# One scan per slot over two units in a decoder layer's state-space scan stage

## The reference, cut to what matters

```python
x = silu(conv(in_proj @ hidden) + conv_b)          # (4, 512 channels, 512 steps)
dt_low, Bm, Cm = split(x_proj @ x)                 # 16 + 16 + 16 rows
dt = softplus(dt_proj @ dt_low + dt_b)
def step(state, inp):                              # over the 512 time steps
    d, b, c, u = inp
    dA = exp(d[..., None] * A)                     # decay, 16 states per channel
    state = state * dA + (d * u)[..., None] * b[:, None, :]
    return state, einsum('bdn,bn->bd', state, c)
y = (ys + D * x) * silu(z)                         # z: the normed residual stream
```

## Time and profile before

| | us |
|---|---|
| median of three runs | 1161.83 (1160.21 to 1162.95) |
| the profiled execution, its own time | 1163.83 |
| its span, first to last instruction | 1162.1 |
| PE, DVE, ACT, POOL busy in the span | 1067.5, 826.7, 666.0, 678.5 |
| scan stage, first to last scan | 148.7 to 646.7 |

### The profile page before, as it was taken

The page is one execution under the profiler, slowest core; times in us unless marked ns, Lnnn a source line. Parts: engine busy times, 40 slices in busy tenths (PEclk is TensorE's granted clock), DMA queues, the critical chain, the costliest instruction groups (busy, mean ns, idle before and its releaser), DMA issues. The chain is left out here.

```text
span 1162.1 us, 19085 instructions
## 1 busy us (share of the span) xinstructions
PE 1067.5 (92%) x6650; PEld 651.8 (56%) x6650; DVE 826.7 (71%) x1244; ACT 666.0 (57%) x1442; POOL 678.5 (58%) x587
## 2 busy tenths in 40 slices
PE   7999978888888888888888999999999989999994
PEld 3454545656556556656665544444444467777761
DVE  6988689999999999999999486640680134434428
ACT  3767789999999999999999324202011012333320
POOL 3022299999999999999999450202043035555530
PEclk9999979999999999999999999999999989999997
DMA  7310111101111111112231043102225424444229
GB/s 217 93 38 13 27 28 38 37 28 38 37 38 28 38 38 33 33 38 80 85 110 47 1 146 109 73 37 72 73 78 199 166 75 135 135 131 132 75 74 387
DMA packets 51966, 94.75 MB, mean 82 GB/s; under 512 B 9950, under 2 KB 18142, under 8 KB 51872
## 3 DMA queue, kind: packets, MB, share of 16 engines
q1 hardware_dynamic: 44352, 72.82, 19.5%
q0 software_dynamic: 7520, 20.72, 5.7%
HBM read 74.51 MB, written 20.84 MB: 82 GB/s over the span
## 5 line engine op out<-in xcount | busy, mean ns | idle before, releaser
L699 POOL TENSOR_TENSOR w_all<-w_all 128x512 f32<-128x512 f32 x256 | 320.5, 1275 | 16.2 <-POOLq L96 16.2
L925 DVE TENSOR_TENSOR_SCAN w_all<-da,w_all 128x512 f32<-128x512 f32 x256 | 298.1, 1205 | 1.1 <-POOL w_all L699 0.9
L857 ACT ACTIVATE da<-w_all,a_flat 128x512 f32<-128x512 f32 x256 | 180.3, 705 | 2.3 <-DVE w_all L925 1.6
L793 PE MATMUL yb<-ident,w_all 128*128 128x128 f32 x1024 | 160.4, 280 | 20.9 <-DVE acc L933 20.7
L865 ACT ACTIVATE w_all<-sc,neg_max 128x128 f32<-128x128 f32 (+3 forms) x256 | 134.3, 541 | 15.7 <-DVE neg_max L917 14.7
L793 PEld LDWEIGHTS yb<-ident,w_all 128*128 128x128 f32 x1024 | 115.6, 142 | 45.6 <-issue 23.9
L743 PE MATMUL sc<-w_all,attn 32*128 32x384 f32 (+3 forms) x512 | 105.6, 489 | 27.2 <-ACT w_all L865 21.9
L1352 POOL TENSOR_TENSOR w_all<-w_all 128x512 f32<-128x512 f32 x24 | 29.4, 1226 | 156.1 <-ACT w_all L1548 156.1
L874 ACT ACTIVATE w_all<-tb 128x256 f32<-128x256 f32 (+2 forms) x192 | 103.0, 536 | 27.8 <-PE tb L758 27.7
L917 DVE TENSOR_REDUCE neg_max<-sc 128x2 f32<-128x256 f32 (+3 forms) x128 | 104.1, 813 | 19.9 <-PE sc L746 15.8
L1874 DVE COPY attn<-w_all 128x512 f32 x94 | 40.3, 429 | 108.2 <-PE pe L1815 106.7
(11 more groups left out here) (222 smaller groups left out, 1651.4 us busy)
## 6 DMA issues: line engine op xcount, KB each, us to landing
w_all<-b_scratch SPq DMA_DIRECT2D x64, 256.0 KB, 3.3
w_all<-in_w_up SPq DMA_DIRECT2D x16, 512.0 KB, 5.5
w_all<-in_w_down SPq DMA_DIRECT2D x16, 512.0 KB, 6.7
w_all<-sorted_y SPq DMA_DIRECT2D x16, 512.0 KB, 10.0
attn<-in_x SPq DMA_DIRECT2D x4, 1024.0 KB, 6.9
w_all<-in_x SPq DMA_DIRECT2D x16, 256.0 KB, 4.3
norms<-attn SPq DMA_DIRECT2D x4, 1024.0 KB, 4.3
out_dram<-acc SPq DMA_DIRECT2D x16, 256.0 KB, 9.3
```

What stands on the lines that cost most here:

```text
L699: pool.tensor_tensor(dbu[:, k, :], keep["du"][i // N][:, k * T:(k + 1) * T], b_all[i % 2][:, :], ALU.mult).then_inc(pool_dbu.sem, pool_dbu ...
L793: last = pe.transpose(yb[which][:, k * P:(k + 1) * P], state[i % 2][:, k, t * P:(t + 1) * P], ident[:, :])
L857: act.activation(da[unit % 2][:, :], keep["dt"][i // N][:, k * T:(k + 1) * T], ACT.Exp, scale=keep["a_flat"][:, unit % (N * KD):unit % (N ...
L925: dve.tensor_tensor_scan(state[i % 2][:, k, :], da[unit % 2][:, :], dbu[:, k, :], 0.0, ALU.mult, ALU.add).then_inc(dve_scan.sem, dve_scan. ...
```

## The change

The two scan units of a slot become one pair. `weigh`, `scan` and the waits on them count pairs (128), `decay` still counts units (256). Three things change:

- one scan of 1024 steps per slot runs over both units. The element of the decays at step 512 is set to 0 once at the start, by a DVE memset, and `decay` of the second unit writes only its steps 1 to 511, so the second unit starts afresh;
- the decays lie in two sets of two units: set 0 in two neighbouring PSUM banks (`da_bank`), set 1 in SBUF (`da_sb`). Even pairs use PSUM, odd pairs SBUF. A `decay` waits for the scan two pairs before, and ACT's order moves each decay half a slot ahead (three before the loop);
- POOL forms both products of a pair in one instruction of 128 x 1024, with the row of b read twice (a broadcast of 2).

```diff
-        da = [pb(f"da{i}") for i in range(2)]
+        da_bank = ctx.enter_context(nc.psum_tensor("da", [P, 2 * T], F32))
+        da_sb = sb("da_sb", [P, 2 * T])
+        da = [da_bank[:, :], da_sb[:, :]]
...
-        out_bank = [sc[:, 0, :], sc[:, 1, :], da[0][:, :], da[1][:, :]]
+        out_bank = [sc[:, 0, :], sc[:, 1, :], da_bank[:, 0:T], da_bank[:, T:2 * T]]
...  SP
-                sp.wait_ge(pool_dbu.sem, pool_dbu.upto(4 * (i - 2) + 3))
+                sp.wait_ge(pool_dbu.sem, pool_dbu.upto(2 * (i - 2) + 1))
...  GpSimd
-                if unit >= 4:
-                    pool.wait_ge(dve_scan.sem, dve_scan.upto(unit - 4))
-                pool.tensor_tensor(dbu[:, k, :], keep["du"][i // N][:, k * T:(k + 1) * T], b_all[i % 2][:, :], ALU.mult).then_inc(...)
+                if pair >= 2:
+                    pool.wait_ge(dve_scan.sem, dve_scan.upto(pair - 2))
+                pool.tensor_tensor(dbu[:, k:k + 2, :], keep["du"][i // N].rearrange("p (k t) -> p k t", t=T)[:, k:k + 2, :],
+                                   b_all[i % 2].rearrange("p (a t) -> p a t", a=1).broadcast_to([P, 2, T]), ALU.mult).then_inc(...)
...
             weigh(0)
-            weigh(1)
             for g in range(UNITS + 3):
                 if g + 1 < UNITS:
-                    weigh(2 * g + 2)
+                    weigh(g + 1)
                 if 0 <= g - 3 < UNITS:
                     add(g - 3)
-                if g + 1 < UNITS:
-                    weigh(2 * g + 3)
...  TensorE
-                    pe.wait_ge(dve_scan.sem, dve_scan.upto(4 * i + 3))
+                    pe.wait_ge(dve_scan.sem, dve_scan.upto(2 * i + 1))
...  ScalarE, decay(unit)
-                if unit >= 2:
-                    act.wait_ge(dve_scan.sem, dve_scan.upto(unit - 2))
-                act.activation(da[unit % 2][:, :], keep["dt"][i // N][:, k * T:(k + 1) * T], ACT.Exp,
+                if unit < 4 and unit % 2 == 0:
+                    act.wait_ge(dve_zero.sem, dve_zero.upto(pair))
+                if pair >= 2:
+                    act.wait_ge(dve_scan.sem, dve_scan.upto(pair - 2))
+                first = unit % 2
+                act.activation(da[pair % 2][:, first * T + first:(first + 1) * T], keep["dt"][i // N][:, k * T + first:(k + 1) * T], ACT.Exp,
...
             decay(0)
             decay(1)
+            decay(2)
...  in the loop
-                    decay(2 * g + 2)
+                    decay(2 * g + 3)
...
-                if g + 1 < UNITS:
-                    decay(2 * g + 3)
+                if g + 2 < UNITS:
+                    decay(2 * g + 4)
...  VectorE, scan(pair)
-                dve.wait_ge(act_da.sem, act_da.upto(unit))
-                dve.wait_ge(pool_dbu.sem, pool_dbu.upto(unit))
+                dve.wait_ge(act_da.sem, act_da.upto(2 * pair + 1))
+                dve.wait_ge(pool_dbu.sem, pool_dbu.upto(pair))
...
-                dve.tensor_tensor_scan(state[i % 2][:, k, :], da[unit % 2][:, :], dbu[:, k, :], 0.0, ALU.mult, ALU.add).then_inc(...)
+                dve.tensor_tensor_scan(state[i % 2][:, k:k + 2, :].rearrange("p k t -> p (k t)"), da[pair % 2],
+                                       dbu[:, k:k + 2, :].rearrange("p k t -> p (k t)"), 0.0, ALU.mult, ALU.add).then_inc(...)
...
+            for n in range(2):
+                dve.memset(da[n][:, T:T + 1], 0.0).then_inc(dve_zero.sem, dve_zero.tick(n))
...
-                    scan(2 * g)
-                    scan(2 * g + 1)
+                    scan(g)
```

More of the change, by code:

```diff
@@ L632, in mix @@
         act_da, act_p, act_turn, act_cy = [signal("act_" + n) for n in ("da", "p", "turn", "cy")]
-        dve_max, dve_scan, dve_acc, dve_rinv, dve_out = [signal("dve_" + n) for n in ("max", "scan", "acc", "rinv", "out")]
+        dve_max, dve_scan, dve_acc, dve_rinv, dve_out, dve_zero = [signal("dve_" + n) for n in ("max", "scan", "acc", "rinv", "out", "zero")]
         pool_dbu, pool_acc, pool_du, pool_xb = [signal("pool_" + n) for n in ("dbu", "acc", "du", "xb")]
         pe_out = signal("pe_out")
-        out_bank = [sc[:, 0, :], sc[:, 1, :], da[0][:, :], da[1][:, :]]
+        out_bank = [sc[:, 0, :], sc[:, 1, :], da_bank[:, 0:T], da_bank[:, T:2 * T]]
         x1 = keep["x1"][0]
@@ L668, in preload @@
                 if n == 0:
-                    sp.wait_ge(pool_dbu.sem, pool_dbu.upto(3 * N * KD - 1))
+                    sp.wait_ge(pool_dbu.sem, pool_dbu.upto(3 * N * KD // 2 - 1))
                     sp.wait_ge(act_da.sem, act_da.upto(3 * N * KD - 1))
@@ L689, in last_batch, with weigh @@
                 pool.tensor_tensor(du, dt, du, ALU.mult).then_inc(pool_du.sem, pool_du.tick(j))
-            def weigh(unit):
-                i, k = unit // KD, unit % KD
-                if unit == (B - 1) * N * KD:
+            def weigh(pair):
+                i, k = pair // 2, 2 * (pair % 2)
+                if pair == (B - 1) * N * KD // 2:
                     pool.wait_ge(pool_du.sem, pool_du.upto(KD - 1))
@@ L696, in weigh @@
                     pool.wait_ge(s_b_all[i % 2].sem, s_b_all[i % 2].upto(i // 2))
-                if unit >= 4:
-                    pool.wait_ge(dve_scan.sem, dve_scan.upto(unit - 4))
-                pool.tensor_tensor(dbu[:, k, :], keep["du"][i // N][:, k * T:(k + 1) * T], b_all[i % 2][:, :], ALU.mult).then_inc(pool_dbu.sem, pool_dbu.tick(unit))
+                if pair >= 2:
+                    pool.wait_ge(dve_scan.sem, dve_scan.upto(pair - 2))
+                pool.tensor_tensor(dbu[:, k:k + 2, :], keep["du"][i // N].rearrange("p (k t) -> p k t", t=T)[:, k:k + 2, :],
+                                   b_all[i % 2].rearrange("p (a t) -> p a t", a=1).broadcast_to([P, 2, T]), ALU.mult).then_inc(pool_dbu.sem, pool_dbu.tick(pair))
             def add(n):
@@ L802, in project_out @@
                     if n == 2 * KD:
-                        pe.wait_ge(dve_scan.sem, dve_scan.upto(2 * UNITS - 1))
+                        pe.wait_ge(dve_scan.sem, dve_scan.upto(UNITS - 1))
                     last = pe.matmul(out_bank[t], keep["attn"][:, 0, k * T + t * P:k * T + (t + 1) * P], keep["wo"][:, k, :],
@@ L853, in decay @@
             def decay(unit):
-                i, k = unit // KD, unit % KD
-                if unit >= 2:
-                    act.wait_ge(dve_scan.sem, dve_scan.upto(unit - 2))
-                act.activation(da[unit % 2][:, :], keep["dt"][i // N][:, k * T:(k + 1) * T], ACT.Exp,
+                i, k, pair = unit // KD, unit % KD, unit // 2
+                if unit < 4 and unit % 2 == 0:
[4 more added lines that the diff above has]
+                act.activation(da[pair % 2][:, first * T + first:(first + 1) * T], keep["dt"][i // N][:, k * T + first:(k + 1) * T], ACT.Exp,
                                            scale=keep["a_flat"][:, unit % (N * KD):unit % (N * KD) + 1]).then_inc(act_da.sem, act_da.tick(unit))
@@ L917, in top, with scan @@
                 dve.tensor_reduce(neg_max[unit % 2][:, :], sc[:, :, 0:n], AX.X, ALU.max, negate=True).then_inc(dve_max.sem, dve_max.tick(unit))
-            def scan(unit):
-                i, k = unit // KD, unit % KD
-                dve.wait_ge(act_da.sem, act_da.upto(unit))
-                dve.wait_ge(pool_dbu.sem, pool_dbu.upto(unit))
+            def scan(pair):
+                i, k = pair // 2, 2 * (pair % 2)
+                dve.wait_ge(act_da.sem, act_da.upto(2 * pair + 1))
+                dve.wait_ge(pool_dbu.sem, pool_dbu.upto(pair))
                 if k == 0 and i >= 2:
                     dve.wait_ge(pe_y.sem, pe_y.upto(4 * (i - 2) + 3))
-                dve.tensor_tensor_scan(state[i % 2][:, k, :], da[unit % 2][:, :], dbu[:, k, :], 0.0, ALU.mult, ALU.add).then_inc(dve_scan.sem, dve_scan.tick(unit))
+                dve.tensor_tensor_scan(state[i % 2][:, k:k + 2, :].rearrange("p k t -> p (k t)"), da[pair % 2],
+                                       dbu[:, k:k + 2, :].rearrange("p k t -> p (k t)"), 0.0, ALU.mult, ALU.add).then_inc(dve_scan.sem, dve_scan.tick(pair))
             def weigh_c(n):
```

## The result

The changed kernel takes 1244.87 us (median of 4 runs, 1243.18 to 1246.51) against 1161.93 for the kernel before (median of 4): ratio 1.0715, 95% interval 1.0696 to 1.0735, 83 us slower. Its profiled execution spans 1241.4 us. The forecast was 1251 (1228 to 1285).

The account below looks back on a forecast made before the run. In the scan stage, POOL with the odd scan it gives way to becomes the bound: 9.2 us for two slots against 7.8, 64 x 1.4 = +90 on 1163.8, less about 1 and then 2.0, gives 1251 us (1228 to 1285).

Parts of the forecast that it names:

- Where the operands lie: Scan stage: odd scans with both inputs in SBUF and POOL instructions reading SBUF exclude each other whole, whoever is first.
- three instructions of DVE after the stage: L1203, L1205, L1206 after the scan stage: beside two-SBUF-input DVE instructions, POOL's L1352 took 2.43 us instead of 1.041.
- A: Rival in odd scans: the scan doesn't take the shared interface, POOL goes on; 1154 us or no change; chance 0.08.
- The sum: Scan stage, two slots: POOL's 7.16 us plus odd scan's 2.12 less 0.1 make 9.2 against 7.8; +90 us.
- the hidden start: When DVE and POOL exclude each other, about 0.15 us at the start of the waiting instruction is hidden.
- the 2.02 that the sum had: POOL's added time per odd scan: the scan's 2.12 us less 0.1 for POOL's own hidden start.
- POOL as the bound: POOL with the odd scan becomes the bound, busy about 100% of a stage of 585 to 590 us.
- The cover of the other edits: ACT's decays, SP's b row, PE's waits and scan source memory cost 0; two memsets under 0.5 us together.
- B: Rival in odd scans: only the scan's accesses are taken from POOL, costing 1.06 us each; 1189 us; chance 0.08.
- C: Rival: odd scans come just after POOL begins a product; DVE's wait bounds, 9.9 us per two slots; 1296; chance 0.09.
- the 1.8 that DVE could afford: DVE has 7.4 us of its own in two slots of 9.2, so can wait 1.8 in the odd slot.

Follow-up runs that it names:

- run 8: The changed kernel with POOL's addition of cy to acc cut to one column instead of 512; 1189.74 us.
- run 3: The changed kernel's paired scan and product, but one set of decays only, in SBUF, issued where the kernel before had them; 1372.52 us.
- run 4: The same kernel and schedule as run 3, but with the one set of decays in PSUM; 1243.01 us.
- run 7: The changed kernel with its one scan and two sets, but two products of 512 for one of 1024; 1262.27 us.
- run 6: The changed kernel with its sets and paired product, but two scans of 512 instead of one of 1024; 1272.2 us.
- run 5: The kernel of run 4 with ACT issuing both decays of the next pair one after the other; 1223.59 us, ratio 1.0528.

## Why the prediction was right

**Where the operands lie.** It rested on three instructions of DVE after the stage. The prediction calls them two operations (a product and a comparison), but both are the same instruction, TENSOR_TENSOR, and no scan was among them. That a scan does the same was a bet, as the prediction says under A, and it came out. What they showed holds for the scan: 2.28 us alone, exclusive with POOL's products and additions, whole, whoever is first. It is shown now by the 51 odd scans that end 2.15 us after a POOL instruction, by the one-column addition of run 8, and by runs 3 and 4 (129.5 us apart for the memory alone). The Trainium skill, page "SBUF — State Buffer", section "Who interferes with whom", has this rule for VectorE instructions with two SBUF inputs; the runs agree for the scan.

**The sum.** For two slots it said 9.2 us: measured 9.10 ((726.3 - 148.3) / 127 x 2). Of its terms, the scan was put at 2.27 and is 2.28 to 2.29; the product at 2.35 from start to start and is 2.33 (412.74 to 415.07), the addition at 1.23 and is 1.22 to 1.24. With these, 2 x (2.33 + 1.23) + 2.12 - 0.1 = 9.14. The rest is the hidden start. A scan that waited ends 2.15 after POOL's end, so 0.13 of it is hidden, as the sum had within 0.03; but a POOL product that waited ends 2.15 after the scan where it takes 2.36 alone, so 0.21 of it is hidden and not 0.15, and 0.04 would be hidden behind another POOL instruction. That gives 7.12 + 2.15 - 0.17 = 9.10, as measured. The stage was to grow by 90 us and grew by 82.3: 1.31 us for two slots instead of 1.4. POOL's waits inside its instructions come to 64 x 1.95 us (128 products of 3.076 on average instead of 2.364, 64 additions of 1.801 instead of 1.272: 91.1 + 33.9 = 125 us), near the 2.02 that the sum had. Of these 125 us not all became time: without them POOL is busy for 453 us, which is 45 less than the 498 of the old stage, and 125 - 45, with 2 us in which POOL is idle, is the growth.

**POOL as the bound.** It is 99.6% busy, as said, of a stage of 580 us that was to have 585 to 590; a load added in run 7 lengthens the stage, one taken away in run 8 shortens it.

**The cover of the other edits.** ACT and PE were to be under 80% and are at 81% and 82%; neither became the bound. ACT's decay into SBUF takes 721 ns and into PSUM 692, on average 707 against the 705 of before, so the 0 holds. PE's waits were put at 0 more and its busy time was left as it was; both were wrong. Its weight loads waited 40.5 us for scans, against 0.8 before, and its busy time rose by 40 us (below). That this cost nothing rests on POOL being the fuller engine. The Trainium skill, page "VectorE: DVE Perf Modes", section on the TRN2 errata, has a source in SBUF 62 cycles of 0.96 GHz cheaper than one in PSUM, by estimate 65 ns. This isn't seen: the shortest scan from SBUF took 2279 ns, the shortest from PSUM 2267.

**The rivals.** A (the scan stays out of it) and B (only its accesses are taken) fall with the one-column addition that waits 2 us. C (DVE's wait becomes the bound) didn't happen: an odd scan waited 0.74 us on average (3.025 against 2.286), of the 1.8 that DVE could afford. A bound of that kind appears in run 8, once POOL's load is gone, as DVE at 98%, and in run 6.

**What the experiments' expectations missed.** That splitting the scan would change nothing (run 6, 27 us), and what one set in PSUM costs through ACT's order (runs 4 and 5). What a merged scan is worth in PSUM stays open. As a length the scan of 1024 saves DVE 0.04 us a slot (2.29 against the 2.33 of two), where the prediction had 0.06; no run shows what that is worth in time.

## What to carry to other kernels

Before a buffer that a VectorE instruction reads is moved from PSUM to SBUF, count its SBUF inputs. With two of them, the scan here and GpSimd's instructions that read SBUF ran one after the other. GpSimd then lost 64 x 1.95 = 125 us inside its instructions, and what its slack of 45 us didn't absorb became time, for 0.06 us a slot to be gained. Whether one long instruction does less harm than two short ones depends on what GpSimd runs beside it: one scan instead of two was 27 us better beside the long product and 2 us, within the noise, beside two short ones. Look for the damage in the maximum of each line's duration, since no wait shows it.

## What the runs showed of the hardware that was not expected

PE's granted clock fell in the stage: 0.91 of full speed against 0.99, for the same 4122 matmuls, and PE's busy time rose from 437 to 477 us. In windows of 2 us (PE busy with its count, clock, DMA share, GB/s):

```profile
404.00:406.00 2.00, 0.45 (x2) 0.87 0.00 0
406.00:408.00 2.00, 2.00 (x16) 0.50 0.38 81
408.00:410.00 2.00, 2.00 (x14) 0.77 0.22 50
```

From 403.79 to 405.55 PE stood still, waiting for DVE's sum L938. Then it worked at 0.50, the lower of its two levels (1.2 GHz), for about 3 us, and from 410 at 1.00 (2.4 GHz) again. The same stands at 420 to 426 us: there the transposes waited 2.2 us for the odd scan of 416.70, which took 4.10, and the clock behind it was 0.64 and 0.51. Waits of PE on DVE are longer than before: for the sum L938 64.4 us against 20.7 for the matmuls of the transposes and 37.5 against 20.9 for their weight loads, and for the scan 40.5 us in 33 waits, up to 2.3 at once, against 0.8. So in these rows a stall of DVE is followed by a slower PE as well. It can hardly have cost time here, because POOL was idle for only 2 us of the stage. In the run with every scan from SBUF the clock of the stage is 0.82.
